# Transposed x kept as two halves, and the halves of the attention sums one turn later

## The reference

```python
xn   = layernorm(x);  x_in = concat([mem, xn])                 # per sequence
q,k,v = x_in@wq.T, x_in@wk.T, x_in@wv.T                        # 4 heads of 64
swa  = softmax(mask(q@k.T/8, window 128)) @ v @ wo.T
pred = silu(x_in@w1.T + b1) @ w2.T + b2                        # 256 -> 1024 -> 256
grads of 0.5*sum((pred-swa)**2) for w1,b1,w2,b2;  p' = (1-alpha)*p - theta*grad
out_mem = silu(x_in@w1'.T + b1') @ w2'.T + b2'
x1   = x + sigmoid(swa@lin1.T)*swa + sigmoid(out_mem@lin2.T)*out_mem
out  = x1 + routed feed-forward (8 experts, top 2, capacity 640) of layernorm(x1)
```

## Time and profile before

| | us |
|---|---|
| median of 3 runs (lowest, highest) | 2566.94 (2564.03, 2571.04) |
| the profiled execution | 2563.92 |
| its span | 2562.1 |
| PE busy | 2427.1 (95%) |
| DVE busy | 1833.0 (72%) |
| ACT busy | 1288.7 (50%) |
| POOL busy | 1343.6 (52%) |
| granted clock, mean | 0.985 |

### The profile page before, as it was taken

One profiled execution on the slowest core, in us unless ns is written; L12 is line 12 of the kernel. 1 busy time (PEld: TensorE's weight loads), 2 busy tenths in 40 slices (PEclk: granted clock), 3 DMA queues, 4 the chain that ended last, 5 costly groups with the idle time before them and its releaser, 6 DMA issues. The chain is left out here.

```text
span 2562.1 us, 41058 instructions
## 1 busy us (share of the span) xinstructions
PE 2427.1 (95%) x15649; PEld 2156.8 (84%) x15649; DVE 1833.0 (72%) x3835; ACT 1288.7 (50%) x2259; POOL 1343.6 (52%) x810
## 2 busy tenths in 40 slices
PE   6999999799999999999999979999999969999998
PEld 5877887589888889998888867777777759999998
DVE  6888887576777777777676666666666666777766
ACT  3777777644444444444444435565565523444333
POOL 2344344456666666666666633666666643343333
PEclk9999999999999999999999989999999979999999
DMA  3222221340101000000000032322222134444441
GB/s 121 65 87 75 67 81 61 123 170 26 34 26 30 25 26 25 25 26 27 32 30 21 18 120 69 97 95 84 86 82 74 37 123 132 133 137 136 151 141 56
DMA packets 135284, 190.33 MB, mean 74 GB/s; under 512 B 13426, under 2 KB 103959, under 8 KB 134960
## 3 DMA queue, kind: packets, MB, share of 16 engines
q1 hardware_dynamic: 121264, 157.27, 18.9%
q0 software_dynamic: 13824, 30.44, 3.6%
HBM read 123.13 MB, written 72.12 MB: 76 GB/s over the span
## 5 line engine op out<-in xcount | busy, mean ns | idle before, releaser
L690 POOL TENSOR_TENSOR prob<-prob,softmax_small 128x1024 f32<-128x1024 f32 x65 | 124.6, 1917 | 243.4 <-DVE softmax_small L614 243.4
L2112 POOL TENSOR_TENSOR m_hl<-m_hf,m_hh 128x512 fp32r<-128x512 f32 x112 | 168.9, 1521 | 145.7 <-ACT m_hh L1775 145.5
L2473 POOL DMA_INDIRECT out<-e_ys,slot_token x80 | 83.1, 1039 | 231.4 <-DVE e_ys L2429 222.2
L104 PE MATMUL e_ps_y<-r_w_h,e_hl 128*128 128x256 f32 x640 | 181.1, 283 | 0.0
L104 PE MATMUL e_ps_y<-r_w_l,e_hh 128*128 128x256 f32 x640 | 179.0, 280 | 0.0
L104 PE MATMUL e_ps_y<-r_w_h,e_hh 128*128 128x256 f32 x640 | 178.9, 280 | 0.0
L822 POOL DMA_INDIRECT xbuf_d<-xn,scatter_rows x128 | 151.5, 1183 | 47.4 <-issue 38.1
L2362 ACT ACTIVATE e_hf<-e_ps_z,e_b 128x640 f32<-128x640 f32 x128 | 102.0, 797 | 147.1 <-PE e_ps_z L104 140.3
L104 PE MATMUL e_ps_z<-slotsT_h,w_l 128*128 128x320 f32 x512 | 159.1, 311 | 1.3 <-DVE slotsT_l L2407 1.3
L104 PE MATMUL e_ps_z<-slotsT_l,w_h 128*128 128x320 f32 x512 | 159.0, 310 | 0.0
L104 PE MATMUL e_ps_z<-slotsT_h,w_h 128*128 128x320 f32 x512 | 158.8, 310 | 0.0
(11 more groups left out here) (305 smaller groups left out, 9016.1 us busy)
## 6 DMA issues: line engine op xcount, KB each, us to landing
shared_x<-in_x SPq DMA_DIRECT2D x32, 512.0 KB, 5.1
shared_xT<-xT_d SPq DMA_DIRECT2D x64, 256.0 KB, 4.8
new_w1T<-in_W SPq DMA_DIRECT2D x16, 1024.0 KB
new_w2T<-in_W SPq DMA_DIRECT2D x16, 1024.0 KB
xbuf_d<-new_w1T SPq DMA_DIRECT2D x16, 650.0 KB, 8.0
slots<-xbuf_d SPq DMA_DIRECT2D x15, 650.0 KB
xn_d<-xn SPq DMA_DIRECT2D x32, 256.0 KB, 2.5
xT_d<-shared_xT SPq DMA_DIRECT2D x32, 256.0 KB, 2.5
```

Source lines behind the costliest of these rows:

```text
L104: i = e.matmul(out, a, b, start=first and not onto and n == 0, stop=last and n == len(terms) - 1, skip_group_check=onto)
L690: e.tensor_tensor(p[:], p[:], sm[:, 3].unsqueeze(2).broadcast_to([P, HEADS, 2 * P]), ALU.mult).then_inc(*prob_made(g))
L2112: e.tensor_tensor(hl[:, t, 0:N], hf[(HC * C + t) % NZ][:, 0:N], hh[:, t, 0:N], ALU.subtract).then_inc(*h_low(C, t))
L2473: e.indirect_dma_start(io["out"], bass.IndirectOffsetOnAxis(ap=token[i % 2][:, b:b + 1], axis=0), ys[:, b], None, bounds_check=NT - 1, oob ...
```

## The change

`xT` no longer exists in float32. ScalarE rounds the transposed x straight from PSUM into the high half, VectorE subtracts from PSUM for the low half; GpSimd has no part in it. Both halves are stored and loaded, as twice as many DMAs, into two buffers `shared.xT` that attention uses as its first probability buffers; the gradient and merge use them as they are, without any rounding. b1 gets a buffer of its own. In attention, round_av and rest_av of block a-4 come in turn a (before: of a-3), on ScalarE at the head of the turn, on VectorE behind maxima(a) and invert(a-1). TensorE's list in attention, and its waits for `av_low`, are unchanged. In the gradient's opening forward(1, 0) comes ahead of transpose_h(0, 1), and the halves of xn of pairs 0 and 1 are made inside the first turn of the loop instead of ahead of it. Cut to its core:

```diff
 class Shared:
-        self.xT = [sb(f"shared_xT{i}", [P, KC * GRP * P]) for i in range(2)]
+        self.xT = [sb(f"shared_xT_{k}", [P, KC * GRP * P], F32R) for k in ("h", "l")]
+        self.b1 = sb("shared_b1", [P, HID])
     def pair_xT(self, i):
-        return self.xT[0][:, i * n:(i + 1) * n].rearrange("p (k t) -> p k t", k=KC)
+        return [t[:, i * n:(i + 1) * n].rearrange("p (k t) -> p k t", k=KC) for t in self.xT]
 # attention
-            return {"x": xT_full, "qk": qk_low, "v": v_low, "o": out_full}[kind].at(*key)
+            return {"x": xT_low, "qk": qk_low, "v": v_low, "o": out_full}[kind].at(*key)
 # attention, ScalarE
-            def copy_x(G, h):
+            def round_x(G, h):
                 act.wait_ge(*tx_done.at(G, h))
-                act.wait_ge(*xT_out[slot(G)].at(before(G), min(1, blocks(before(G)) - 1)))
-                act.wait_ge(*xT_low.at(before(G), min(1, blocks(before(G)) - 1)))
-                e.activation(xT[slot(G)][:, :, cols], ps_x[:, :, 0:n * P], ACTF.Copy).then_inc(*xT_full(G, h))
+                act.wait_ge(*xT_out[slot(G)].at(before(G), min(1, blocks(before(G)) - 1), 1))
+                act.wait_ge(*final_use(before(G)))
+                e.activation(xTh[slot(G)][:, :, cols], ps_x[:, :, 0:n * P], ACTF.Copy).then_inc(*xT_high(G, h))
             for a in TURNS:
                 early, late = steps_at(a)
+                if a - 4 in turns:
+                    round_av(a - 4)
                 for kind, *key in early:
                     do[kind](*key)
                 if a - 2 in turns:
                     round_pt(a - 2)
                 if a in turns:
                     soft(a)
-                if a - 3 in turns:
-                    round_av(a - 3)
 # attention, VectorE
-            def round_x(G, h):
-                dve.wait_ge(*xT_full.at(G, h))
-                dve.wait_ge(*final_use(before(G)))
-                e.tensor_copy(xTh[s][:, :, cols], xT[s][:, :, cols]).then_inc(*xT_high(G, h))
+            def rest_x(G, h):
+                dve.wait_ge(*xT_high.at(G, h))
+                e.tensor_tensor(xTl[s][:, :, cols], ps_x[:, :, 0:n * P], xTh[s][:, :, cols], ALU.subtract).then_inc(*xT_low(G, h))
                     maxima(a)
                 if a - 1 in turns:
                     invert(a - 1)
+                if a - 4 in turns:
+                    rest_av(a - 4)
                 for kind, *key in early:
                     do[kind](*key)
                 if a - 2 in turns:
                     rest_pt(a - 2)
-                if a - 3 in turns:
-                    rest_av(a - 3)
 # attention, GpSimd: rest_x and its calls are gone
 # attention, SP
-                sp.wait_ge(*xT_full.at(G, h))
-                e.dma_start(io["xT_d"][2 * G + h][:, :, 0:n * P], xT[s][:, :, cols]).then_inc(*xT_out[s](G, h))
+                for part, (made_x, src) in enumerate(((xT_high, xTh), (xT_low, xTl))):
+                    sp.wait_ge(*made_x.at(G, h))
+                    e.dma_start(io["xT_d"][part][2 * G + h][:, :, 0:n * P], src[s][:, :, cols].bitcast(F32)).then_inc(*xT_out[s](G, h, part))
-                    sp.wait_ge(*xT_out[0].at(NGRP - 2, 1))
-                    sp.wait_ge(*xT_low.at(NGRP - 2, 1))
-                    e.dma_start(shared.pair_xT(0), io["xT_d"][0]).then_inc(*next_xT(0))
-                    sp.wait_ge(*xT_out[1].at(NGRP - 1, 1))
-                    sp.wait_ge(*xT_low.at(NGRP - 1, 1))
-                    e.dma_start(shared.xT[1][:], io["b1"]).then_inc(*next_b1(0))
+                    e.dma_start(shared.b1[:], io["b1"]).then_inc(*next_b1(0))
+                if a == NBLK + 1:
+                    sp.wait_ge(*xT_out[0].at(0, 1, 1))
+                    sp.wait_ge(*av_done.at(NBLK - 2))
+                    for p in range(2):
+                        for part in range(2):
+                            e.dma_start(shared.pair_xT(p)[part].bitcast(F32), io["xT_d"][part][p]).then_inc(*next_xT(p, part))
 # gradient, TensorE
             forward(0, 0)
             forward(0, 1)
             transpose_h(0, 0)
+            forward(1, 0)
             transpose_h(0, 1)
-            forward(1, 0)
             predict(0)
 # gradient, ScalarE and VectorE: round_xT, rest_xT and all their calls are gone; round_xn and rest_xn
-            round_xn(0)
-            round_xn(1)
             for p in range(1, PAIRS + 1):
                 ...
+                if p == 1:
+                    round_xn(0)
+                    round_xn(1)
                 if now:
                     round_dT(p)
-                if p == PAIRS:
-                    act.wait_ge(*chunk_in[0].at(0, final_pair(0)))
-                    act.wait_ge(*pred_done.at(NPAIR))
-                    e.activation(halves[0][:, 0:KC * T], shared.xT[0][:], ACTF.Copy).then_inc(*chunk_high(0))
-                if p == PAIRS:
-                    dve.wait_ge(*chunk_high.at(0))
-                    e.tensor_tensor(halves[1][:, 0:KC * T], shared.xT[0][:], halves[0][:, 0:KC * T], ALU.subtract)
 # gradient, SP
-                sp_.wait_ge(*xT_low.at(p - 2))
-                e.dma_start(xT_f[s][:, :, 0:n * P], io["xT_d"][p][:, :, 0:n * P]).then_inc(*xT_in[s](p))
+                sp_.wait_ge(*z_done.at(2 * p - 3, 1))
+                for part, xT in enumerate((xTh, xTl)):
+                    e.dma_start(xT[s][:, :, 0:n * P].bitcast(F32), io["xT_d"][part][p][:, :, 0:n * P]).then_inc(*xT_in[s](p, part))
-                    sp_.wait_ge(*xT_low.at(NPAIR))
-                    load_chunk(e, io, shared, chunk_in, 0)
-                    sp_.wait_ge(*seeded.at(TILES - 1, 1))
-                    load_chunk(e, io, shared, chunk_in, 1)
+                    sp_.wait_ge(*z_done.at(TILES - 1, 1))
+                    load_chunk(e, io, shared, halves, chunk_in, 0)
+                    sp_.wait_ge(*pred_done.at(NPAIR))
+                    load_chunk(e, io, shared, halves, chunk_in, 1)
 # merge: round_xT and rest_xT are gone; TensorE waits for the load itself; SP
-                    sp.wait_ge(*xT_low.at(C))
-                    load_chunk(e, io, shared, chunk_in, C + 2)
+                    sp.wait_ge(*z_done.at(C, HC - 1))
+                    load_chunk(e, io, shared, halves, chunk_in, C + 2)
```

More of the change, by code:

```diff
@@ L255, in attention_phase @@
         small = [sb(f"softmax_small{i}", [P, 4, HEADS]) for i in range(NPR)]
-        pth = [sb(f"probT_h{i}", [P, 2, HEADS, P], F32R) for i in range(2)]
-        ptl = [sb(f"probT_l{i}", [P, 2, HEADS, P], F32R) for i in range(2)]
+        pth, ptl = ([t[:].rearrange("p (b h t) -> p b h t", b=2, h=HEADS), sb(n, [P, 2, HEADS, P], F32R)]
+                    for n, t in zip(("probT_h1", "probT_l1"), shared.xT))
         ah = [sb(f"attnT_h{i}", [P, KC, GRP * P], F32R) for i in range(2)]
@@ L283, in attention_phase @@
         xn_out = [signal(f"xn_out{i}", pairs[i], 16) for i in range(2)]
-        xT_out = [signal(f"xT_out{i}", pairs[i], 16) for i in range(2)]
+        xT_out = [signal(f"xT_out{i}", [(*u, part) for u in pairs[i] for part in range(2)], 16) for i in range(2)]
         w2T_in = [signal(f"w2T_in{k}", [0], 16) for k in range(2)]
@@ L883, in columns, with chunk_xT, load_chunk @@
     return slice(blocks.start * P, blocks.stop * P)
-def load_chunk(e, io, shared, chunk_in, C):
-    xT = shared.xT[C % 2][:].rearrange("p (k t) -> p k t", k=KC)
+def chunk_xT(shared, halves, C):
+    return [t[:, 0:KC * T].rearrange("p (k t) -> p k t", k=KC) for t in (halves if C % 2 else shared.xT)]
+def load_chunk(e, io, shared, halves, chunk_in, C):
     for h, pair in chunk_pairs(C):
-        e.dma_start(xT[:, :, 2 * h * P:(2 * h + 2) * P], io["xT_d"][pair]).then_inc(*chunk_in[C % 2](C, h))
+        for part, xT in enumerate(chunk_xT(shared, halves, C)):
+            e.dma_start(xT[:, :, 2 * h * P:(2 * h + 2) * P].bitcast(F32), io["xT_d"][part][pair]).then_inc(*chunk_in[C % 2](C, h, part))
 def gradient_phase(nc, io, sems, shared, halves, g1, g2, b1n, b2n, first_xT, b1_in, oT_out, chunk_in):
@@ L922, in gradient_phase @@
         xn_f = [sb(f"xn_f{i}", [P, 2, D]) for i in range(2)]
-        xT_f = [shared.pair_xT(i) for i in range(2)]
         oT_f = [sb(f"oT_f{i}", [P, KC, 2 * P]) for i in range(2)]
@@ L926, in gradient_phase @@
         xnl = [sb(f"xn_l{i}", [P, 2, D], F32R) for i in range(2)]
-        xTh, xTl = sb("g_xTh", [P, KC, 2 * P], F32R), sb("g_xTl", [P, KC, 2 * P], F32R)
+        xTh, xTl = zip(*(shared.pair_xT(i) for i in range(2)))
         hh = [sb(f"h_h{i}", [P, HID], F32R) for i in range(4)]
@@ L949, in gradient_phase @@
             signal(n, [0], 16) for n in ("g_ident_in", "g_scale_in", "g_b2_in", "g_rates_in", "g_b1c_in"))
-        xT_in, xn_in, oT_in = ([signal(f"g_{n}_in{i}", [p for p in pairs if p % 2 == i and (p or n != "xT")], 16)
-                                for i in range(2)] for n in ("xT", "xn", "oT"))
+        xT_in = [signal(f"g_xT_in{i}", [(p, part) for p in pairs[2:] if p % 2 == i for part in range(2)], 16) for i in range(2)]
```

(19 more changed lines are left out.)

81 lines of the change are left out of this document (22 added, 59 removed).

## The result

| | before | after |
|---|---|---|
| median (lowest, highest), 4 runs each | 2568.36 (2564.03, 2571.04) | 2598.55 (2597.77, 2600.8) |
| the profiled execution, its span | 2563.92, 2562.1 | 2598.25, 2596.5 |
| PE, DVE, ACT, POOL busy | 2427.1, 1833.0, 1288.7, 1343.6 | 2434.8, 1718.8, 1253.0, 1263.5 |

A forecast was written before the change was run, and what follows sets the result against it. TensorE was taken as bound (attention 317 of 340 us, gradient 64.00 of 64), a new loop slowing attention. -1.5 + 33 + 7 - 5.9 - 1.0 = +31.6 gave 2595.5 or 2598.5; forecast 2597 us, range 2574 to 2612.

The forecast's parts named there:

- Steady attention: Attention from turn 4 to 56: each group of four turns 30.4 us against 27.65, together +33 (0 to +38).
- the 13 us for its upper end: Steady attention: extra cost if VectorE's subtraction from PSUM took as long as the cast, 1.26 us, instead of 0.6 to 0.69.
- The floor: Steady attention: with VectorE always waiting for the scores, 3.58 us from scores to attend, so even at best 27.65 a group.
- the ring: Attention: closed loop in every turn of scores(a), maxima(a), rest_av(a-4), attend(a-3); 7.6 us attend to attend where TensorE needs 6.2.
- Rival B: Attention: the new wait at attend does not bind and both old waits vanish, -25, total 2533; chance 0.10.
- Tail and end: Attention's turns 56 to 63 and its last outputs, slower through the new loop: +7 (+1 to +10).
- Start: Start of attention: turn 4 begins about 1.5 us earlier (3 earlier to 1 later), turn 1 not waiting for GpSimd.
- Opening: The gradient's opening: xT preparations and TensorE's waits of 3.21 and 3.52 us go, -5.9 (-7 to -2).
- The 3.5 for the xn halves: Gradient's opening: with the xn halves covered by predict(1), TensorE's 3.52 us wait for the first dz halves goes.
- rival C: Attention: TensorE's clock falls to 0.90 in the new gaps, +14, total 2611; chance 0.07.
- Gradient to merge: VectorE's serial chain from the last g1 sums to the new w1 loses L1376 (1.22 us): -1.0.
- Merge: Merge phase: rounding of xT lies off TensorE's waits and doubled loads have time, 0 (-1 to +2).

The follow-up runs named there:

- e1: The kernel before with only round_av and rest_av of block a-4 moved to turn a; 2612.39 us, ratio 1.0174.
- e2: The changed kernel with round_av and rest_av of block a-3 back in turn a, in their old places; 2548.9 us, ratio 0.9929.
- e3: The changed kernel with VectorE's rest_av(a-4) ahead of maxima(a) instead of behind it; 2544.1 us, ratio 0.9904.
- e6: The changed kernel again, unchanged, run for its merge phase; 2600.48 us.
- e4: e2 with the xn halves of pairs 0 and 1 ahead of the gradient's loop again; 2552.95 us.
- e7: e2 with forward(1, 0) behind transpose_h(0, 1) again; 2554.1 us.
- e9: e5 with VectorE's first_term of chunk C-1 ahead of the first hidden step of chunk C in merge; 2530.14 us, ratio 0.9853.
- e11: e3 again, unchanged, in another set of runs, for its merge phase; 2544.26 us.
- e5: e3 with round_av and rest_av of block a-3 in their old places from turn 56 on; 2544.22 us, ratio 0.9904.
- e12: e5 again, unchanged, in another set of runs; 2536.64 us, ratio 0.9881.

## Why the prediction was right, and where its sizes were off

**Steady attention, +33 against +30.15.** The mechanism and its place are shown by e1, e2 and e3. The working had 7.2, 7.6, 7.6 and 8.0 for the four steps; measured are 6.96, 7.54, 7.54 and 8.02. The excess is in the step from the first to the second turn, and in the 27.65 to which it was compared: 13 groups before average 27.73. The subtraction from PSUM, in the trace after, is 1.29 for two in a row, 0.645 from one to the next, within the 0.6 to 0.69 taken, so the 13 us for its upper end do not arise:

```profile
200.14 1.29 DVE L584 TENSOR_TENSOR w_l<-ps_proj,w_h 128x512 fp32r<-128x512 f32 x2
```

**The floor.** That "even at best a group stays 27.65" is worked out for this order of VectorE's list, and no run here reached it. It is no floor for the delay by a turn as such: with the ring open the old waits and most of the new one go, 26.43. Rival B had the place and two thirds of the price: e3's steady part is 16.9 under the kernel before, against B's 25, and it takes rest_av ahead of maxima to get there.

**Tail and end, +7 against +7.2.** Within bounds; e6 and e1 have +9.1.

**Start, -1.5 against +0.75.** Turn 0 itself begins 2.0 later (49.28 against 47.30), which was not in the sum. All other traces have that (48.6 to 50.0), e1 too, where x is made as before; its cause is open, and the one trace of before may be the odd one. From turn 0 to 4 the changed kernel gains 1.2, with one stretch at the 1.2 GHz level of about 3 us (from 69.2 us, behind a wait of 2.08), where the kernel before has two (from 48.2 and 55.0). e2, without the ring and at 1.00, gains 5.0.

**Opening, -5.9 against -8.8.** This term was mis-sized by 2.9 and lies outside its -7 to -2. Of the 8.8, 4.1 lie ahead of the first dT transposes (29.5 us before, 25.5 after; forecast 2.4) and 4.8 between the first and the second (27.2, 22.4; forecast 3.5). The 3.5 for the xn halves was priced as the wait alone. It took the clock with it: 4.3 to 5.1 in e4, and in the kernel before, behind its 3.52, TensorE was slowed in the same way (busy, instructions, clock):

```profile
534.00:544.00 10.00, 7.63 (x52) 0.83 0.39 137
```

The 2.4 ahead of it counted on the order of forward(1, 0), and e7 shows that the order gives nothing; the preparations of xT gave 4.1 in the changed kernel and 5.4 in e2 and e7, with the clock (0.83 over that stretch before, 0.87 and 0.93 after).

**Clock, rival C.** It did not come: the clock was 1.00 from 90 to 533 us, with a gap of 0.5 to 1.1 us in every turn of steady attention and of 1.56 in the tail's. (Ahead of that it fell once in the steady stage, for about 3 us at 86.2, behind a wait of 1.93.) The Trainium skill (TensorE: Matmul & The Clock Gate, "HAM oscillation — how this bites in real kernels") describes waits that recur between groups of matmuls and bring the clock down each time. The trace here doesn't show that of its shorter gaps: the many of 0.5 to 1.1 us did no harm. Single longer ones did: 2.48 us in e4, 3.21 and 3.52 in the kernel before.

**Gradient to merge, -1.0.** Measured -1.6 from the second dT transposes on, of which 0.6 are 32 pairs at 30.19 instead of 30.21.

**Merge, 0 against +7.25.** Five late sigmoids, which are not the change's. At 1.4 each they make 7.1 of the 7.25. In e2 to e4, which have none, the phase is 1.7 shorter than before, which is 0.7 outside -1 to +2. So of the 34.3 us between the two profiled executions 25 to 27 are the change's, against 31.6 forecast: start +2.3, steady -2.9, tail +0.2, opening -2.9, the new weights -0.6, merge 0 to -1.7 and the experts -0.5 off. The median of before is 4.4 above its profiled execution, that of after 0.3; the forecast took 1.5 for that, and with the late sigmoids this brought the median to 2598.6, so near 2597 partly by chance.

## What to carry to other kernels

Work that frees a single buffer of the bounding engine must not stand, in its engine's list, behind an instruction that waits for that same engine's current turn; check it by walking from the buffer's writer to its releaser and asking what each link waits for. Delaying such work by a turn was a gain in steady attention once it headed the turn (26.43 against 27.65 a group), and a loss in the tail (67.8 to 71.1 against 59.1). A removed stall of some microseconds on TensorE is worth more than its length where the granted clock fell behind it. And where VectorE and GpSimd both work from SBUF, who starts first decides: in this kernel it paid to put VectorE's long instruction in its idle time ahead of GpSimd's.

The best version here is e9: x as halves, rest_av at the head of the turn (old order from turn 56 on), first_term early. It takes 2530.14 us, 1.5% less than the kernel before.

## What the runs showed of the hardware

- After standstills of 2.48 (e4), 3.21 and 3.52 us (the kernel before) in the gradient's opening TensorE worked at the 1.2 GHz level for about 3 us, though its queue was full (0.50 and 0.74 in two stretches of 2 us, e4). After one of 2.04 to 2.06 us in that opening the clock fell in e4, e6, e9 and e11 and stayed at 1.00 in e2, e3, e5 and e12, and after one of 2.7 us in the tail it stayed at 1.00 in the kernel before, so the length alone doesn't decide. Gaps of up to 1.1 us every 7.5 left the clock at 1.00.
- Two subtractions of 128x512 in a row with one input in PSUM took 1.29 us on VectorE. A product of 128x1024 with both inputs in SBUF took 1.22 when it started ahead of GpSimd's subtraction, 2.27 when GpSimd had started 0.10 before.
- ScalarE started an instruction some 0.5 us late with its input done (0.41 to 0.61), at the same five places of the program in four traces (the changed kernel's two, e5 and e7), and nowhere in those of e1 to e4, e9, e11 and e12.
